# Turning the attended tiles of a gated cross-attention kernel by DMA in two 16-bit planes, with ScalarE joining and VectorE rounding

## Chip, cores and metric

The kernel runs on 1 core of a Trainium2 chip, as one launch. The metric is the device time of that launch in microseconds.

## What is computed

`x` and `ctx` are 64 sequences of 128 positions with 256 features, float32. The block is a gated cross-attention followed by a gated feed-forward layer in which each token uses 4 of 16 blocks.

```python
def attend(Q, K, V):                      # 16 heads of 16 features, causal
    scores = jnp.einsum('bhqd,bhkd->bhqk', q, k) * scale
    scores = jnp.where(causal_mask, scores, jnp.finfo(scores.dtype).min)
    return jnp.einsum('bhqk,bhkd->bhqd', softmax(scores), v)
def ffn(x):                               # 1024 hidden units in 16 blocks of 64
    prob = softmax(x @ w_router + b_router)
    mask = the 4 blocks of highest prob, per token
    h = relu(x @ w1.T + b1)
    return (h * mask) @ w2.T + b2
x = x + tanh(g_xattn) * attend(layernorm(x), ctx, ctx)
x = x + tanh(g_ffn) * ffn(layernorm(x))
```

## The kernel before, in words

The work goes by tiles: tile b is one sequence, 128 positions on the partitions and 256 features in the free dimension. The feed-forward part takes two tiles (a pair) at a time. The program is written out engine by engine. Each engine runs its own list of instructions in order, and the lists are tied by semaphores with constant targets. One loop over `ITERATIONS` (i from -4 to 71) is written on every engine; in iteration i, for example, scores of tile i+1, shifted scores of tile i, the output of attention for tile i-1, the transposes of tile i-2's second normalisation, and the feed-forward part of earlier tiles are issued. Nothing but these lists and waits sets the order of the work.

**Attention.** VectorE takes mean and variance of x (`layernorm_stats`, L622) and POOL makes the reciprocal root of the variance as a power of -0.5 on one number per partition (`rstd_of`, L792: L794 adds epsilon, L796 takes the power). VectorE normalises into `q_pad` (L637). The queries have to be turned so that the features lie on the partitions. From tile 9 on, and from tile 7 on for the keys, this is done without TensorE: POOL splits the float32 numbers into a plane of low and a plane of high 16-bit halves (`query_parts` L815, `key_parts` L807), SyncE issues a transposing DMA of the planes (`queries_spread` L929, `keys_spread` L939), and ScalarE joins the planes again by a copy on 16-bit numbers (`q_joined` L498, `k_joined` L504). Each of these moves 256 KB, 1024 16-bit numbers a partition. TensorE computes the scores (L302, L315), VectorE the row maxima (L647, L649), which travel two tiles later in a spare column of the queries. When ScalarE has joined the queries of tile i+2, SyncE moves the maxima of tile i into the rows of tile i's queries by two small DMAs (`max_row`, L921, issues at L925). Only when they have landed can TensorE compute `shifted_scores(i)` (L332), whose exponentials ScalarE takes (L513). POOL zeroes what is not causal (`causal_weights`, L830), and TensorE multiplies with the values (`attention_out`, L345) into bank M0, from which ScalarE copies (L519). After another turn (L359) VectorE divides, gates and adds x (`attention_added`, L652 to L667) and takes the statistics of the result x2.

**From x2 to the feed-forward part, which is what changes.** POOL makes the root of x2's variance (the same `rstd_of`, at the head of its iteration) and then `x_b` (L873). VectorE normalises x2 into `xn` (`normalised_again`, L672). TensorE turns `xn` by two 128x128 transposes (`x_transposed`, L370) into bank M0. ScalarE copies that bank twice (`x_copies`, in `rest`, the last thing of its iteration before the second hidden part): as float32 into `xT` for the router (L525), and rounded to the reduced type fp32r into `xT_high` (L528). VectorE subtracts the two into `xT_low` one iteration later (`x_parts`, L678). The hidden layer multiplies high by high, low by high and high by low (L411 to L413), and the output layer likewise (L434 to L436).

**The router** runs in even iterations i, for the pair whose second tile is i-3. TensorE makes the logits from `xT` (L381, `router_logits`) ahead of `attention_out`, waiting for `x_copied` of that second tile. ScalarE copies them (L593), TensorE turns them (L389), VectorE picks the blocks (`route`, L713 to L729), ScalarE makes `used` (L544), and in the next, odd, iteration SyncE turns `used` by a transposing DMA (`used_spread`, L965), which stands in its list ahead of `max_row`.

**The order in one iteration**, as far as it matters here:

```python
# SyncE:   used_spread (odd i); max_row(i); queries_spread(i+3); keys_spread(i+3); loads (even i); store (odd i)
# ScalarE: k_joined(i+2); logits copy (even i); out_copied(i-1); exponentials(i); hidden_parts(m);
#          choice (even i); q_joined(i+3); x_copies(i-2); hidden_parts(m+1)
# VectorE: finished; attention_added(i-2); normalised(i+3); row_maximum(i+1); hidden_masked(m);
#          normalised_again(i-2); layernorm_stats(i+4); x_parts(i-3); route (even i); hidden_masked(m+1)
# POOL:    root of x2(i-2); x_b; hidden_low; query_parts; values; key_parts; root of x(i+4);
#          causal_weights(i); hidden_low
```

## Time and profile before

| | us |
|---|---|
| median of 3 runs (694.48 to 695.71) | 695.15 |
| span of the profiled execution | 694.6 |
| PE busy | 671.8 |
| POOL busy | 564.2 |
| VectorE (DVE) busy | 519.7 |
| ScalarE (ACT) busy | 511.9 |

The profile gives for the profiled execution the span from its first to its last instruction; what lies around it is not in it. Busy times are unions over an engine's instructions; matmuls are pipelined and their ends are modelled, so where the price of a matmul matters the distance from one start to the next says more than the duration. DMA-issuing instructions of SyncE stand in its timeline (SPq) with the time that issuing took, and are not counted as busy.

### The profile page before, as it was taken

The numbers are of one execution on the slowest core, as the hardware profiler recorded it, in microseconds if no ns is written. First come the engines' busy times: TensorE is split into PE (matmuls) and PEld (weight loads), VectorE is DVE, ScalarE is ACT, GpSimd is POOL, SyncE is SP. The second block draws the span as 40 slices with busy tenths as digits, with TensorE's granted clock in tenths as the row PEclk, the third lists the DMA queues.
The fourth block names the chain that finished last, engine by engine and source line by source line (L and its number), as shares of the span: only waits on it lengthen the run. The fifth ranks groups of instructions, "written<-read, shape, count | busy, mean of one in ns | idle before, by whom it ended". The sixth has DMA issues, their size and how long they took to land.

```text
span 694.6 us, 30557 instructions
## 1 busy us (share of the span) xinstructions
PE 671.8 (97%) x13072; PEld 623.5 (90%) x13072; DVE 519.7 (75%) x1429; ACT 511.9 (74%) x785; POOL 564.2 (81%) x778
## 2 busy tenths in 40 slices
PE   6779999999999999999999999999999999999998
PEld 5668899999999999999989999999999999999997
DVE  6788877877777787787787787778777777877752
ACT  3657787787787878778778777877877877786642
POOL 5687889889888888988988988898898888886642
PEclk9989999999999999999999999999999999999999
DMA  5322345444335354344444444533533544342010
GB/s 162 95 78 39 83 114 75 106 113 80 95 101 110 86 99 113 79 82 113 113 79 103 105 72 99 114 95 86 113 83 82 110 113 77 75 83 50 20 38 32
DMA packets 161814, 61.90 MB, mean 89 GB/s; under 512 B 135696, under 2 KB 161424, under 8 KB 161680
## 3 DMA queue, kind: packets, MB, share of 16 engines
q1 hardware_dynamic: 160848, 58.38, 37.7%
q8 instruction: 104, 1.70, 1.1%
q10 hardware_dynamic: 832, 1.57, 0.8%
q14 instruction: 30, 0.25, 0.1%
HBM read 19.03 MB, written 8.39 MB: 39 GB/s over the span
## 4 chain that ended last, share of the span: by engine, by line
PE 87%; DVE 4%; POOL 3%; SPq 2%; DMA 1%; issue 1%; ACT 1%; POOLq 0%; DVEq 0%
PE bank L411 10%; PE score_banks L332 10%; PE score_banks L302 8%; PE bank L413 8%; PE bank L412 8%; PE bank L436 8%; PE bank L435 8%; PE bank L434 8%; PE bank L345 8%; PE bank L359 4%; PE bank L370 3%; PE bank L381 1%; PE score_banks L315 1%; DMA qT<-qT 1%; PE bank L389 1%
## 5 line engine op out<-in xcount | busy, mean ns | idle before, releaser
L837 POOL TENSOR_TENSOR h_low<-hid,h_high 128x512 fp32r<-128x512 f32 x128 | 164.8, 1287 | 12.8 <-ACT hid L535 12.6
L709 DVE SCALAR_TENSOR_TENSOR hid<-bank,b_cols,used_all 128x256 f32<-128x256 f32 x248 | 108.2, 478 | 73.0 <-PE bank L413 66.9
L513 ACT ACTIVATE weights<-score_banks 128x1024 f32<-128x1024 f32 x128 | 124.3, 1023 | 40.3 <-PE score_banks L332 40.3
L411 PE MATMUL bank<-xT_high,w_high 128*128 128x256 f32 x496 | 150.7, 304 | 0.3 <-DVE hid L709 0.2
L830 POOL TENSOR_SCALAR_AFFINE_SELECT weights<-weights 128x1024 f32<-128x1024 f32 x128 | 138.3, 1105 | 8.6 <-ACT weights L513 8.2
L413 PE MATMUL bank<-xT_high,w_low 128*128 128x256 f32 x496 | 139.2, 281 | 0.0
L412 PE MATMUL bank<-xT_low,w_high 128*128 128x256 f32 x496 | 139.1, 280 | 0.0
L434 PE MATMUL bank<-w_high,h_high 128*128 128x256 f32 x488 | 137.3, 281 | 0.7 <-POOL h_low L837 0.7
L436 PE MATMUL bank<-w_high,h_low 128*128 128x256 f32 x488 | 138.0, 283 | 0.0
L435 PE MATMUL bank<-w_low,h_high 128*128 128x256 f32 x488 | 137.5, 282 | 0.0
L794 POOL TENSOR_SCALAR ve<-mv 128x1 f32<-128x1 f32 x128 | 34.6, 271 | 89.9 <-DVE mv L620 89.8
L411 PEld LDWEIGHTS bank<-xT_high,w_high 128*128 128x128 f32 x496 | 93.3, 188 | 4.7 <-issue 0.6
L412 PEld LDWEIGHTS bank<-xT_low,w_high 128*128 128x128 f32 x496 | 93.7, 189 | 0.0
L413 PEld LDWEIGHTS bank<-xT_high,w_low 128*128 128x128 f32 x496 | 93.3, 188 | 0.0
L434 PEld LDWEIGHTS bank<-w_high,h_high 128*128 128x128 f32 x488 | 92.0, 189 | 0.9 <-POOL h_low L837 0.9
L436 PEld LDWEIGHTS bank<-w_high,h_low 128*128 128x128 f32 x488 | 91.9, 188 | 0.0
L435 PEld LDWEIGHTS bank<-w_low,h_high 128*128 128x128 f32 x488 | 91.8, 188 | 0.0
L534 ACT ACTIVATE h_high<-hid 128x512 fp32r<-128x512 f32 x128 | 82.4, 644 | 9.2 <-DVE hid L709 9.2
L519 ACT COPY oT<-bank 128x512 f32<-128x512 f32 x64 | 37.6, 587 | 67.1 <-PE bank L345 67.1
L501 ACT COPY qT<-qT_parts 128x1024 uint16<-128x1024 uint16 x57 | 77.6, 1361 | 9.0 <-DMA qT_parts<-q_parts 8.6
L332 PE MATMUL score_banks<-qT,kT 32*128 32x128 f32 x2048 | 76.0, 285 | 7.7 <-DVE q_pad L649 4.3
L332 PEld LDWEIGHTS score_banks<-qT,kT 32*128 32x128 f32 x2048 | 63.8, 188 | 20.8 <-issue 13.9
(102 smaller groups left out, 1508.4 us busy)
## 6 DMA issues: line engine op xcount, KB each, us to landing
x_in<-in_x SPq DMA_DIRECT2D x31, 256.0 KB, 3.3
out_y<-y_out SPq DMA_DIRECT2D x31, 256.0 KB, 2.4
c_in<-in_ctx SPq DMA_DIRECT2D x30, 256.0 KB
qT<-qT SPq DMA_DIRECT2D x128, 4.0 KB
w_stage<-in_w1T ACTq DMA_DIRECT2D x1, 1024.0 KB, 5.9
hid<-in_w2T SPq DMA_DIRECT2D x8, 128.0 KB, 2.7
kT_parts<-k_parts SPq DMA_TRANSPOSE x57, 2.8
qT_parts<-q_parts SPq DMA_TRANSPOSE x57, 2.7
```

The lines of the kernel that those rows point to most:

```text
L332: made = pe.matmul(out=score_banks[:, u, cols], lhsT=kT[rows, s, cols], rhs=qT[rows, s, cols], start=True, stop=True, tile_position=(u * P ...
L411: pe.matmul(out=bank, lhsT=w1_high[:, k, c], rhs=high, start=k == 0, stop=False)
L412: pe.matmul(out=bank, lhsT=w1_high[:, k, c], rhs=low, start=False, stop=False)
L413: made = pe.matmul(out=bank, lhsT=w1_low[:, k, c], rhs=high, start=False, stop=k == KC - 1)
L434: pe.matmul(out=bank[:, 0:D], lhsT=high, rhs=w2_high[:, c, :], start=a, stop=False)
L435: pe.matmul(out=bank[:, 0:D], lhsT=high, rhs=w2_low[:, c, :], start=False, stop=False)
L436: made = pe.matmul(out=bank[:, 0:D], lhsT=low, rhs=w2_high[:, c, :], start=False, stop=z)
L513: act.activation(weights[:, b % 2, half * 2 * HB:(half + 1) * 2 * HB, :].rearrange("p h q -> p (h q)"), score_banks[:, 2 * half:2 * half + ...
L534: act.activation(h_high[:, p % 2, chunks], hid[:, n % 4], ACT.Relu)
L709: dve.scalar_tensor_tensor(hid[:, n % 4, j], hid_bank(n)[:, j * TOKS:(j + 1) * TOKS], b1_cols[:, c:c + 1], used_all[:, p % 2], ALU.add, AL ...
L830: pool.affine_select(out=w, in_=w, compare_op=ALU.is_ge, fill=0.0, base=0, pattern=[[0, 2 * HB], [1, S]], channel_multiplier=-1).then_inc( ...
L837: pool.tensor_tensor(h_low[:, p % 2, chunks], hid[:, n % 4], h_high[:, p % 2, chunks].bitcast(F32), ALU.subtract).then_inc(h_low_made, 1)
```

## The change

- **Turning by DMA.** Tiles 6 to 61 (`x_by_pe` is false) are not turned by TensorE. POOL splits `xn` into two 16-bit planes (`x_split`, behind `key_parts` and ahead of `causal_weights`, waiting for `xn_made`). At the head of the next iteration SyncE issues a transposing DMA of 128x512 16-bit numbers (`x_turned_by_dma`), and ScalarE joins the planes into `xT` (`x_joined`), behind `k_joined` and ahead of the logits' copy. For these tiles both PSUM copies go. Tiles 0 to 5, 62 and 63 are still turned by TensorE and copied to `xT` by ScalarE.
- **Rounding.** For all tiles `xT_high` is now made by VectorE from `xT` in SBUF, in `x_parts`, just ahead of the subtraction; the wait for `hidden_made` moves with it.
- **Roots in pairs.** One POOL step makes the root for x of tile i+4 and for x2 of tile i-2 together, over two columns, at the head of the iteration. The statistics of x are taken one tile earlier (`layernorm_stats(i + 5)`), and the loop starts one iteration earlier.

The diff, cut to its core (declarations of semaphores and shifted set-up conditions are left out):

```diff
...
-half_power = sb("half_power", [P, 1], F32)
+half_power = sb("half_power", [P, 2], F32)
...
-mv1 = sb("mv1", [P, 2, 2], F32)
-ve1 = sb("ve1", [P, 2, 1], F32)
-rstd1 = sb("rstd1", [P, 2, 1], F32)
+mv = sb("mv", [P, 2, 2, 2], F32)
+ve = sb("ve", [P, 2, 2], F32)
+rstd = sb("rstd", [P, 2, 2], F32)
...
-mv2 = sb("mv2", [P, 2, 2], F32)
-ve2 = sb("ve2", [P, 2, 1], F32)
-rstd2 = sb("rstd2", [P, 2, 1], F32)
...
+xn_parts = sb("xn_parts", [P, 2, 2, D], U16)
+xT_parts = sb("xT_parts", [P, 2, 2, KC, S], U16)
...
+x_spread = [sem(f"x_spread{i}") for i in range(2)]
...
+TURNS_BY_PE = 6
 def q_early(b):
...
 def used_pair(i):
...
-FIRST, LAST = -4, N - 1 + OUT_LAG + 1
+FIRST, LAST = -5, N - 1 + OUT_LAG + 1
+def root_of_x(b):
+    return b - 4 - FIRST
+def root_of_x2(b):
+    return b + 2 - FIRST
+def x_by_pe(b):
+    return b < TURNS_BY_PE or b >= N - 2
...
     def attention_out(b):
-        if b >= 2:
-            pe.wait_ge(xT_high_made, b - 1)
-        elif b >= 1:
+        if b >= 2 and x_by_pe(b - 2):
+            pe.wait_ge(x_copied, b - 1)
+        if b >= 1:
...
         else:
-            pe.wait_ge(xT_high_made, b)
+            pe.wait_ge(x_copied, b)
...
             hidden(p, m + 1)
-        if 0 <= i - 2 < N:
+        if 0 <= i - 2 < N and x_by_pe(i - 2):
...
     def x_copies(b):
...
         turned = banks[M0][:, 0:D].rearrange("p (c s) -> p c s", s=S)
-        act.wait_ge(x_turned, b + 1)
+        act.wait_ge(x_turned, b + 1 if b < TURNS_BY_PE else b - (N - 2) + TURNS_BY_PE + 1)
         act.copy(xT[:, :, t, :], turned).then_inc(x_copied, 1)
-        if t == 0 and p >= 2:
-            act.wait_ge(hidden_made, PIECES * (p - 1))
-        act.copy(xT_high[:, p % 2, :, t, :], turned).then_inc(xT_high_made, 1)
+    def x_joined(b):
+        p, t = divmod(b, PAIR)
+        n, slot = divmod(b - TURNS_BY_PE, 2)
+        act.wait_ge(x_spread[slot], 16 * (n + 1))
+        act.wait_ge(xT_low_made, b - 1)
+        act.wait_ge(routed, p)
+        act.copy(xT[:, :, t, :].bitcast(U16).rearrange("p c (s h) -> p h c s", h=2),
+                 xT_parts[:, slot]).then_inc(x_copied, 1)
...
     def hidden_parts(p, m):
...
     def rest(i):
         p, m = hidden_pair(i)
-        if 0 <= i - 2 < N:
+        if 0 <= i - 2 < N and x_by_pe(i - 2):
...
         weights_high(i)
+        if 0 <= i - 3 < N and not x_by_pe(i - 3):
+            x_joined(i - 3)
         if pr is not None:
...
-    def stats_of(source, stats, mv, s, b, stats_made, mean_made):
-        dve.bn_stats(stats[:, s, :], source).then_inc(stats_made, 1)
+    def stats_of(source, stats, kind, b, stats_made, mean_made):
+        dve.bn_stats(stats[:, b % 2, :], source).then_inc(stats_made, 1)
         dve.wait_ge(stats_made, b + 1)
-        dve.bn_aggr(mv[:, s, :], stats[:, s, :]).then_inc(mean_made, 1)
+        dve.bn_aggr(mv[:, b % 2, kind, :], stats[:, b % 2, :]).then_inc(mean_made, 1)
...
     def layernorm_stats(b):
...
             dve.wait_ge(x_landed[slot], 16 * (n + 1))
-        stats_of(x_in[:, b % XS, :], stats1, mv1, b % 2, b, x_stats, x_mean)
+        stats_of(x_in[:, b % XS, :], stats1, 0, b, x_stats, x_mean)
...
     def normalised(b):
         s = b % 2
-        dve.wait_ge(rstd1_made, b + 1)
+        dve.wait_ge(rstd_made, root_of_x(b))
...
         dve.tensor_scalar(q_pad[:, b % QS, :, 0:HD], x_in[:, b % XS, :].rearrange("p (h d) -> p h d", d=HD),
-                          mv1[:, s, 0:1], rstd1[:, s], ALU.subtract, ALU.mult).then_inc(qn_made, 1)
+                          mv[:, s, 0, 0:1], rstd[:, s, 0:1], ALU.subtract, ALU.mult).then_inc(qn_made, 1)
...
     def row_maximum(b):
...
         dve.wait_ge(x2_made, b + 1)
-        stats_of(x2[:, s], stats2, mv2, s, b, x2_stats, x2_mean)
+        stats_of(x2[:, s], stats2, 1, b, x2_stats, x2_mean)
...
     def normalised_again(b):
         s = b % 2
-        dve.wait_ge(rstd2_made, b + 1)
-        dve.tensor_scalar(xn[:, s], x2[:, s], mv2[:, s, 0:1], rstd2[:, s],
+        dve.wait_ge(rstd_made, root_of_x2(b))
+        if b >= 2 and not x_by_pe(b - 2):
+            dve.wait_ge(x_parts_made, b - 2 - TURNS_BY_PE + 1)
+        dve.tensor_scalar(xn[:, s], x2[:, s], mv[:, s, 1, 0:1], rstd[:, s, 1:2],
...
     def x_parts(b):
         p, t = divmod(b, PAIR)
+        dve.wait_ge(x_copied, b + 1)
+        if t == 0 and p >= 2:
+            dve.wait_ge(hidden_made, PIECES * (p - 1))
+        dve.tensor_copy(xT_high[:, p % 2, :, t, :], xT[:, :, t, :]).then_inc(xT_high_made, 1)
...
             normalised_again(i - 2)
-        if 0 <= i + 4 < N:
-            layernorm_stats(i + 4)
-        if i == FIRST:
+        if 0 <= i + 5 < N:
+            layernorm_stats(i + 5)
+        if i == FIRST + 1:
...
 def _(pool):
-    def rstd_of(mv, ve, result, s, b, mean_made, ve_made, rstd_made):
-        pool.wait_ge(mean_made, b + 1)
-        pool.tensor_scalar(ve[:, s], mv[:, s, 1:2], LN_EPS, None, ALU.add).then_inc(ve_made, 1)
-        pool.wait_ge(ve_made, b + 1)
-        pool.tensor_tensor(result[:, s], ve[:, s], half_power[:], ALU.pow).then_inc(rstd_made, 1)
+    def roots(i):
+        s = i % 2
+        from_x, from_x2 = 0 <= i + 4 < N, 0 <= i - 2 < N
+        if from_x:
+            pool.wait_ge(x_mean, i + 4 + 1)
+        if from_x2:
+            pool.wait_ge(x2_mean, i - 2 + 1)
+        kinds = slice(0 if from_x else 1, 2 if from_x2 else 1)
+        pool.tensor_scalar(ve[:, s, kinds], mv[:, s, kinds, 1], LN_EPS, None, ALU.add).then_inc(ve_made, 1)
+        pool.wait_ge(ve_made, i - FIRST)
+        pool.tensor_tensor(rstd[:, s, kinds], ve[:, s, kinds], half_power[:, kinds], ALU.pow).then_inc(rstd_made, 1)
...
     def values(b):
...
                          ).then_inc(q_parts_made, 1)
+    def x_split(b):
+        n, slot = divmod(b - TURNS_BY_PE, 2)
+        pool.wait_ge(xn_made, b + 1)
+        if n >= 1:
+            pool.wait_ge(x_spread[slot], 16 * n)
+        pool.tensor_copy(xn_parts[:, slot], xn[:, b % 2].bitcast(U16).rearrange("p (d l) -> p l d", l=2)
+                         ).then_inc(x_parts_made, 1)
...
     def causal_weights(b):
...
         p, m = hidden_pair(i)
+        if 0 <= i + 4 < N or 0 <= i - 2 < N:
+            if i + 4 == 0:
+                pool.wait_ge(numbers_set, 1)
+            roots(i)
         if 0 <= i - 2 < N:
             b = i - 2
-            rstd_of(mv2, ve2, rstd2, b % 2, b, x2_mean, ve2_made, rstd2_made)
             if b == 0:
...
             key_parts(i + 3)
-        if 0 <= i + 4 < N:
-            if i + 4 == 0:
-                pool.wait_ge(numbers_set, 1)
-            rstd_of(mv1, ve1, rstd1, (i + 4) % 2, i + 4, x_mean, ve1_made, rstd1_made)
+        if 0 <= i - 2 < N and not x_by_pe(i - 2):
+            x_split(i - 2)
         if 0 <= i < N:
...
         weights_low(i)
-        if i == FIRST + 2:
+        if i == FIRST + 3:
             pool.memset(k_parts[:, :, :, :, HD:], 0).then_inc(parts_zeroed, 1)
...
+    def x_turned_by_dma(b):
+        slot = (b - TURNS_BY_PE) % 2
+        if b - 2 >= TURNS_BY_PE:
+            sync.wait_ge(x_copied, b - 1)
+        sync.wait_ge(x_parts_made, b - TURNS_BY_PE + 1)
+        sync.dma_start_transpose(xT_parts[:, slot].rearrange("p l c s -> p (l c) s"),
+                                 xn_parts[:, slot].rearrange("p l d -> p (l d)")).then_inc(x_spread[slot], 16)
     for i in ITERATIONS:
         pu = used_pair(i)
+        if 0 <= i - 3 < N and not x_by_pe(i - 3):
+            x_turned_by_dma(i - 3)
         if pu is not None:
```

## Rows read from the trace of the kernel before

**Rows 1.** The page: span, and busy time of the engines.

```profile
span 694.6 us, 30557 instructions
PE 671.8 (97%) x13072; PEld 623.5 (90%) x13072; DVE 519.7 (75%) x1429; ACT 511.9 (74%) x785; POOL 564.2 (81%) x778
```

**Rows 2.** Stretches: length, busy PE, PEld, DVE, ACT, POOL, granted clock, DMA.

```profile
20.00:50.00 30.00, 21.71 (x628) 17.88 (x628) 24.52 (x46) 18.35 (x32) 22.98 (x35) 0.95 0.25 64
300.00:400.00 100.00, 99.53 (x2010) 92.69 (x2010) 75.88 (x216) 78.15 (x118) 85.99 (x117) 1.00 0.45 99
```

**Rows 3.** Timeline of PE: start us, duration us, what.

```profile
342.91 0.44 PE L370 MATMUL bank<-ident,xn 128*128 128x128 f32 x2
343.11 0.36 PE L411 MATMUL bank<-xT_high,w_high 128*128 128x256 f32 x1
...
353.11 0.44 PE L370 MATMUL bank<-ident,xn 128*128 128x128 f32 x2
353.38 0.33 PE L389 MATMUL bank<-adding,logitT 128*128 128x64 f32 x2
```

**Rows 4.** Groups of instructions: busy us, mean ns | idle us before, releaser.

```profile
L370 PE MATMUL bank<-ident,xn 128*128 128x128 f32 x128 | 28.2, 302 | 1.0 <-DVE xn L672 1.0
L709 DVE SCALAR_TENSOR_TENSOR hid<-bank,b_cols,used_all 128x256 f32<-128x256 f32 x248 | 108.2, 478 | 73.0 <-PE bank L413 66.9
L796 POOL TENSOR_TENSOR rstd<-ve,half_power 128x1 f32<-128x1 f32 x128 | 73.2, 572 | 10.7
L794 POOL TENSOR_SCALAR ve<-mv 128x1 f32<-128x1 f32 x128 | 34.6, 271 | 89.9 <-DVE mv L620 89.8
L811 POOL COPY k_parts<-c_in 128x512 uint16<-128x512 uint16 x57 | 34.9, 613 | 0.0
```

**Rows 5.** The chain of waits up to the shifted scores of tile 35.

```profile
352.46 1.25 SPq L936
353.81 2.41 SPq L946
...
357.46 1.18 SPq L965
358.69 0.57 SPq L925
359.31 3.43 DMA qT<-qT
```

**Rows 6.** Timeline of SyncE's issues, iterations 29 and 51.

```profile
294.41 0.45 SPq L918 DMA_DIRECT2D x_in<-in_x  x1
295.42 1.18 SPq L965 DMA_TRANSPOSE used_all<-used  x1
296.65 1.15 SPq L925 DMA_DIRECT2D qT<-qT  x2
...
523.25 1.15 SPq L925 DMA_DIRECT2D qT<-qT  x2
```

**Rows 7.** Timeline of PE: shifted scores 29 and 51, router's matmuls of iterations 12 and 36.

```profile
300.95 1.17 PE L332 MATMUL score_banks<-qT,kT 32*128 32x128 f32 x32
...
526.18 0.50 PE L332 MATMUL score_banks<-qT,kT 32*128 32x128 f32 x8
...
126.08 0.43 PE L381 MATMUL bank<-xT,w_router 128*32 128x128 f32 x8
...
371.74 0.43 PE L381 MATMUL bank<-xT,w_router 128*32 128x128 f32 x8
```

**Rows 8.** Timeline of ScalarE, iterations 12 and 35 to 36.

```profile
125.60 1.38 ACT L507 COPY kT<-kT_parts 128x1024 uint16<-128x1024 uint16 x1
...
368.10 0.38 ACT L525 COPY xT<-bank 128x256 f32<-128x256 f32 x1
...
368.62 0.66 ACT L534 ACTIVATE h_high<-hid 128x512 fp32r<-128x512 f32 x1
...
369.67 1.38 ACT L507 COPY kT<-kT_parts 128x1024 uint16<-128x1024 uint16 x1
```

**Rows 9.** Who waited for whom: us in total, times, longest us.

```profile
SPq L925 <- ACT qT L501: 46.7, 30, 3.1
DVE q_pad L637 <- POOL rstd L796: 3.9, 5, 1.0
```

**Rows 10.** VectorE's second normalisation: duration ns min/median/max.

```profile
L672 DVE TENSOR_SCALAR xn<-x,mv,rstd x64: 402/406/1179, 31.6 to 664.7; 128x256 f32<-128x256 f32 x64
```

More of the change, by code:

```diff
@@ L178, in build @@
         x2_stats, x2_mean, xn_made = sem("x2_stats"), sem("x2_mean"), sem("xn_made")
-        ve1_made, ve2_made = sem("ve1_made"), sem("ve2_made")
+        ve_made = sem("ve_made")
         xT_low_made, hid_made, y_made = (sem(n) for n in ("xT_low_made", "hid_made", "y_made"))
@@ L190, in build @@
         v_zeroed, v_ones_set, v_levels_set = sem("v_zeroed"), sem("v_ones_set"), sem("v_levels_set")
-        rstd1_made, rstd2_made = sem("rstd1_made"), sem("rstd2_made")
+        rstd_made = sem("rstd_made")
         v_made, weighted, x2_b2_made = (sem(n) for n in ("v_made", "weighted", "x2_b2_made"))
@@ L194, in build @@
             "parts_zeroed", "parts_ones_set", "parts_levels_set", "k_parts_made"))
+        x_parts_made = sem("x_parts_made")
         q_parts_zeroed, q_parts_made = sem("q_parts_zeroed"), sem("q_parts_made")
@@ L557, in _ @@
             act.wait_ge(numbers_set, 2)
-            act.activation(scratch[:], half_power[:], ACT.Exp)
+            act.activation(scratch[:], half_power[:, 0:1], ACT.Exp)
             act.wait_ge(triangle_made, 1)
@@ L775, in _ @@
                     route(pr)
-                if i == FIRST + 1:
+                if i == FIRST + 2:
                     places(2)
@@ L780, in _ @@
                     hidden_masked(p, m + 1)
-                if i == FIRST + 1:
+                if i == FIRST + 2:
                     dve.wait_ge(ident_made, 1)
@@ L901, in _ @@
                                     ).then_inc(parts_levels_set, 1)
-                if i == FIRST + 3:
+                if i == FIRST + 4:
                     pool.memset(q_parts[:, :, :, :, RIDE_COL + 1:], 0).then_inc(q_parts_zeroed, 1)
```

## Prediction

> **What bounds the kernel now.** I read the page first: PE is busy 97% of the span, the other engines 74 to 81% [rows 1]. That is an average, so I looked at stretches. Between 300 and 400 us PE is busy for 99.53 of 100 us at the full granted clock, between 20 and 50 us for 21.71 of 30 [rows 2]. So for about 570 us TensorE is the bound, and what it no longer has to do comes off the span, unless something else arrives late. The first 80 us are a chain across engines.
>
> Then I asked how close the others are. The chain of waits shows one place in steady state where PE was held up: the two short DMAs of `max_row(35)` landed 3.43 us after their issue began, and what led to them was SyncE's own queue, one transposing DMA after another [rows 5]. SyncE's timeline shows that this is a pattern. In odd iterations it issues query parts, key parts, two loads, `used_all`, and only then `max_row`, back to back; issuing a transposing DMA takes it 1.2 us whatever the size, now and then 2.4 us [rows 5, 6].
>
> **PE.** 56 of 64 tiles (6 to 61) lose two transposes. Busy time says 28.2 us for 128 [rows 4], 0.44 us a tile, but matmuls overlap. From start to start it is 342.91 to 343.11, 0.20 us, in front of the hidden matmuls and 353.11 to 353.38, 0.27 us, in front of the logits' turn [rows 3]. Half the tiles are of each kind: 56 x 0.23 = 12.9 us. Bounds: 56 x 0.20 = 11 and 56 x 0.44 = 25 us; starts decide, so I stay near the low end.
>
> **ScalarE.** The two PSUM copies leave the end of the iteration: 368.10 to 368.62, 0.5 us [rows 8]. `x_joined` comes in behind `k_joined`, ahead of the logits' copy, `out_copied` and the exponentials. The like copy of twice the elements takes 1.38 us [rows 8], so it costs 0.7 to 1.4; I take 0.75, near half. For tiles up to 61 the router's matmuls of the even iteration (L381) now wait for it, where before their copy was made an iteration earlier. Usually `k_joined` ends at 371.05 and L381 starts at 371.74 [rows 7, 8]: 0.69 + 0.5 (key copy earlier) - 0.2 (PE earlier) - 0.75 leaves 0.24 us, no stall. But in six of 26 even iterations the query parts landed late and the key copy too: 125.60 + 1.38 = 126.98, against L381 at 126.08 [rows 7, 8]. There the join ends 0.90 - 0.5 + 0.2 + 0.75 = 1.35 us too late. The other five are later by less, so I charge 6 x 1.0 = 6 us. Bounds: 0, and, if the copy took 1.38, 0.4 x 20 + 2.0 x 6 = 20 us.
>
> **SyncE.** 56 more transposing DMAs, 1.2 us of issue each, stand at the head of iteration i, ahead of `used_spread`, `max_row` and the query and key parts. Their own waits are long over: the split is made on POOL an iteration before. In even iterations it hides: `max_row` waits for ScalarE's copy, 46.7 us in 30 times, 1.6 us each [rows 9]. In odd ones the queue has 0.56 us to spare (294.86 to 295.42) in the row shown [rows 6], 0.0 to 0.6 in 25 others and 1.5 in one, so `max_row` moves by 0.6 to 1.2, about 0.9 us, and PE comes 0.2 earlier. From the end of its issue to the use by L332 there are now 297.80 to 300.95, 3.15 us [rows 6, 7]; over the 27 odd iterations from 9 to 61 the gaps are 1.8 to 3.2, median 3.0. That leaves 1.9. How long does the landing take? At most 1.78 us in iteration 51 (524.40 to 526.18, PE did not wait) [rows 6, 7], and 2.9 us in iteration 35 (359.84 to 362.74) [rows 5]. So the charge is 0 in each if landings are of the first kind and 27 x 1.0 = 27 us if of the second. Only one of 27 is shown to have held PE up, so I stay nearer the low end: 0.22 each, 6 us.
>
> The Trainium skill ("DMA: Bandwidth & Descriptors", section "Issuing engines are not separate DMA queues") says that the time to initiate a DMA is usually small beside the DMA. The trace disagrees for this form: 1.25 us of issue. By the page's word SyncE's charge would be nil.
>
> **VectorE.** It now makes all 64 high parts (128x256, SBUF to SBUF), where it only subtracted. The nearest row is the normalisation of the same size, 402 ns at least, 406 median, 1179 at most [rows 10]; I take 0.4, 26 us in all, and at worst 1.2. It lies between `layernorm_stats` and `route` or `hidden_masked`, which idle for PE anyway: 73.0 us in front of L709 alone [rows 4]. Charge 0; if that idle time were gone it would be 26 us. Its new waits (`x_copied`, and `hidden_made`, which moves here from ScalarE) are met in steady state; behind them queue `route` and the second `hidden_masked`.
>
> That 1179 is a VectorE operation held up by POOL. The Trainium skill ("SBUF — State Buffer", section "Who interferes with whom") has copies and casts in a 2-port mode taking a port pair shared with GpSimd, each blocking the other for a whole instruction. The trace agrees in kind; the added copy falls beside POOL's work, so by the rule POOL loses up to 0.4 us an iteration or VectorE about a microsecond, both within idle time.
>
> **POOL.** Two roots of 0.27 + 0.57 us a tile become one [rows 4], over two columns: 0.57 to 1.14 us for the power; I take 0.6, since the fixed part must be most of it. That saves 0.8 us a tile, and the split (128x512 16-bit, like L811's 0.61 us) gives back 0.6. The split waits for `xn_made`, which holds up the causal selects behind it, but leaves them no later than the second root did: nil. The early place of x's root helps at the start, where VectorE waited 3.9 us for it in five tiles [rows 9] and PE was idle: -2 us, bounds 0 and -4.
>
> **Sum.** 12.9 + 2 gained; 6 + 6 lost, less 1 because a router stall gives the next `max_row` time: -3.9 us. The profiled execution spans 694.6 us, the median is 695.15, 0.5 above; the difference goes on the median: 691.2, say 691.
>
> **Rivals.**
> A, forecast: part of PE's gain is given back at `max_row` and the router: 691. Chance 0.42.
> B, hidden anyway: landings are fast and the joins in time, PE keeps it all: 695.15 - 14.9 = 680. For it: only one stall on a DMA in steady state today. Against: the gaps in odd iterations shrink by a third, and six key copies end after L381. The skill's page on DMA, cited above, leans this way. Chance 0.18.
> C, slower: SyncE's queue becomes the bound of the odd iterations. The x transpose pushes `max_row` by 0.9 us, landings behind loads and transposes take 2.9, PE idles in front of L332. With this in half of the 27, 13.5 us, and 6 at the router: 695.15 - 14.9 + 19.5 = 700. It decides from 0.33 us an odd iteration, (14.9 - 6) / 27. For it: rows 5 show just this chain with the transposing DMAs in it, and there will be more slow issues. Against: a typical landing is under 1.8. Chance 0.27.
> D, gain and loss cancel: 0.33 us an odd iteration: 695. Chance 0.13. That the change does not do what it says has no room: the diff takes the transposes off PE.
>
> Range: from 681, which leaves out the lower part of B, to 701, which leaves out the upper part of C (27 us at `max_row` would give 713). A alone, with its two charges between 3 and 9 us each, spans 684 to 697. No change is within 0.2% (693.8 to 696.5), about what a measurement of this kernel can tell. A gives 0.37 faster and 0.03 each for same and slower, less a little; with B, C and D: faster 0.55, same 0.15, slower 0.30.
>
> **What would show it.** PE should show 16 L370-like transposes where there were 128, and L332 should be waiting for the DMA on qT in odd iterations, by 6 us in sum if A is right, near nothing if B, over 13 if C. L381 waiting for ScalarE, 6 us in about six places, shows the router term; in every even iteration it would mean a copy nearer 1.4 us. ScalarE's join should be 0.75 us, VectorE's high part 0.4, POOL's power 0.6. PE should have less idle time between 20 and 50 us by 2 us. If L411 or L434 wait for VectorE or POOL, my zero charges there are wrong; so is the PE term if the step from L332 to L411 grows.

## Result and profile after

The changed kernel takes 704.79 us (median of 4 runs, 702.76 to 705.86), beside 695.43 for the kernel before in the same session (4 runs, 694.48 to 696.61): a ratio of 1.0131, 95% interval 1.0109 to 1.0153. It is slower by 9.4 us where I forecast 4 us faster, and it lies beyond the range's upper end of 701. The profiled execution spans 704.1 us, 9.5 more than that of before [rows 1].

The page after, span, busy times and the queue that SyncE's DMAs use:

```profile
span 704.1 us, 30581 instructions
PE 664.9 (94%) x12960; PEld 615.2 (87%) x12960; DVE 557.0 (79%) x1493; ACT 517.8 (74%) x721; POOL 554.2 (79%) x718
...
q1 hardware_dynamic: 191312, 65.72, 47.5%
```

PE has 112 matmuls fewer and 6.9 us less to do than in [rows 1], and yet the span is longer: PE now waits. Stretches of the kernel after (length, busy PE, PEld, DVE, ACT, POOL, granted clock, DMA), to be read against [rows 2]:

```profile
20.00:50.00 30.00, 22.39 (x632) 19.36 (x631) 23.54 (x44) 17.91 (x29) 20.69 (x27) 0.90 0.15 42
300.00:400.00 100.00, 97.69 (x1987) 90.46 (x1986) 82.79 (x218) 78.49 (x107) 83.59 (x107) 1.00 0.55 108
90.00:645.00 555.00, 539.45 (x10769) 500.71 (x10768) 451.90 (x1226) 437.27 (x590) 462.69 (x587) 1.00 0.56 106
```

The granted clock in the steady part is full, as before. Between 20 and 50 us it is 0.90 on average, against 0.95 in [rows 2]. In the last stretch PE is idle for 15.5 us; in the kernel before it was idle there for 0.5, as its row of the same stretch shows:

```profile
90.00:645.00 555.00, 554.53 (x10989) 517.16 (x10989) 423.30 (x1187) 434.70 (x654) 474.08 (x640) 1.00 0.43 94
```

Who waited for whom after the change (total us, times, longest):

```profile
PEld score_banks L344 <- DMA qT<-qT: 20.0, 25, 2.3
PE score_banks L344 <- DMA qT<-qT: 12.1, 17, 2.0
...
PEld bank L393 <- ACT xT L545: 6.7, 10, 1.1
...
PE bank L393 <- ACT xT L545: 4.6, 9, 0.9
```

L344 is the line of the shifted scores (L332 before) and L393 that of the router's logits (L381 before). Both waits stand where the prediction named them; one is twice as large as I charged.

**Where the 9.5 us are.** The shifted scores of tile 8 and of tile 63 cut the span in three. PE's timeline after:

```profile
87.60 1.17 PE L344 MATMUL score_banks<-qT,kT 32*128 32x128 f32 x32
...
655.62 1.17 PE L344 MATMUL score_banks<-qT,kT 32*128 32x128 f32 x32
```

and before:

```profile
86.43 1.17 PE L332 MATMUL score_banks<-qT,kT 32*128 32x128 f32 x32
...
647.37 1.17 PE L332 MATMUL score_banks<-qT,kT 32*128 32x128 f32 x32
```

The middle takes 568.0 us instead of 560.9, 7.1 more; the start takes 1.2 more and the tail (48.5 against 47.3) 1.2 more. Among the variants below the start goes from 83.8 to 88.3 and the tail from 46.9 to 48.6, so I attribute neither of these two to a cause.

In the middle, the distance between the shifted scores of neighbouring tiles is 10.20 to 10.23 us before and, where nothing stalls, 10.02 to 10.04 after: PE gains 0.18 to 0.19 a tile, about 10.2 us over 55 tiles. Added up from one start to the next over iterations 9 to 63, the stalls in front of L344 are 12.1 us in 19 places, all in odd iterations (before: 0.5 in one), and those in front of L393 5.4 us in 10 places (before: none). So -10.2 + 11.6 + 5.4 = +6.8 of the 7.1 us. Below, "stalls" are these sums for L344 and L393.

**What delays `max_row`.** SyncE's timeline of the kernel after, iteration 39, with what led up to it (start us, issuing time, line):

```profile
399.12 1.25 SPq L977 DMA_TRANSPOSE qT_parts<-q_parts  x1
400.46 2.35 SPq L987 DMA_TRANSPOSE kT_parts<-k_parts  x1
402.90 0.54 SPq L955 DMA_DIRECT2D c_in<-in_ctx  x1
403.50 0.48 SPq L959 DMA_DIRECT2D x_in<-in_x  x1
404.08 1.20 SPq L1014 DMA_TRANSPOSE xT_parts<-xn_parts  x1
405.37 1.20 SPq L1006 DMA_TRANSPOSE used_all<-used  x1
406.62 1.24 SPq L966 DMA_DIRECT2D qT<-qT  x2
```

The seven issues stand back to back. The small spare time in front of `used_all` that [rows 6] show is gone; the added line L1014 comes before it and pushes all behind it. PE's timeline then has, for shifted scores 39 and 47 (the brackets: idle time before, and the releaser):

```profile
410.16 0.39 PE L344 MATMUL score_banks<-qT,kT 32*128 32x128 f32 x4 [1.57 <-DMA qT<-qT]
...
492.33 0.39 PE L344 MATMUL score_banks<-qT,kT 32*128 32x128 f32 x4 [0.17 <-DMA qT<-qT]
```

In iteration 39 issue ends at 407.86 and PE starts 2.30 us later. In iteration 47 the landing is short, and a slow `used_all` makes the delay instead:

```profile
486.57 1.19 SPq L1014 DMA_TRANSPOSE xT_parts<-xn_parts  x1
487.85 2.13 SPq L1006 DMA_TRANSPOSE used_all<-used  x1
490.04 1.15 SPq L966 DMA_DIRECT2D qT<-qT  x2
```

There issue ends at 491.19, and PE starts 1.14 us later. Of the 19 stalls 11 have a landing of 1.7 to 2.5 us (7.3 us of stall), and eight one of about 1.1 (4.8 us). In each of these eight one issue of the x turn or of `used_all` took 2.1 to 3.2 us (four times each), and in no other of the 28 odd iterations did one of the two take 2 us. Measured from the shifted scores of the tile before, the issue of `max_row` in odd iterations ends at 8.43 us after the change and at 7.16 before (medians of 28): it moved by 1.3 us. Where no issue is slow it goes from 7.06 to about 8.16, by 1.1 us.

**What makes the router late.** In seven of the ten stalls at L393 ScalarE had finished the key copy and waited for the x turn itself to land. In iteration 48, for example (start us, duration us, line; the brackets as above):

```profile
498.69 1.36 ACT L519 COPY kT<-kT_parts 128x1024 uint16<-128x1024 uint16 x1
501.25 0.77 ACT L545 COPY xT<-xT_parts 128x512 uint16<-128x512 uint16 x1 [1.20 <-DMA xT_parts<-xn_parts]
```

SyncE had finished issuing that turn at 498.06, 3.19 us before the join started. In eight of the 26 even iterations from 10 to 60 the join waited in this way, each time until 2.9 to 3.4 us behind the end of the issue. In the other three stalls (iterations 12, 24 and 56) the join followed a late key copy, the case that the prediction had priced.

**The other parts.** One tile's or one line's instructions after (duration in ns, min/median/max):

```profile
L1014 SPq DMA_TRANSPOSE xT_parts<-xn_parts x56: 1188/1214/2371, 92.4 to 657.4; - x56
L545 ACT COPY xT<-xT_parts x56: 754/777/796, 98.4 to 660.8; 128x512 uint16<-128x512 uint16 x56
...
L828 POOL TENSOR_TENSOR rstd<-ve,half_power x70: 567/720/734, 5.2 to 670.9; 128x2 f32<-128x2 f32 x58, 128x1 f32<-128x1 f32 x12
```

and, as groups (busy us, mean ns, idle time before and its releaser), the high part, the split and what is left of the transposes:

```profile
L863 POOL COPY xn_parts<-xn 128x512 uint16<-128x512 uint16 x56 | 35.1, 626 | 4.3 <-DVE xn L694 4.3
L702 DVE CAST xT_high<-xT 128x256 fp32r<-128x256 f32 x64 | 26.8, 419 | 0.2 <-issue 0.2
...
L382 PE MATMUL bank<-ident,xn 128*128 128x128 f32 x16 | 3.7, 315 | 0.7 <-DVE xn L694 0.7
```

### The profile page after: what moved, and what is told of

Read it like the earlier page. It is cut to its first block, busy times and chain, and to the rows that moved or that the text cites. A ratio compares the mean times of both kernels' runs of the same rounds, so it can differ in the third digit from the quotient of the medians.

```text
span 704.1 us, 30581 instructions
## 1 busy us (share of the span) xinstructions
PE 664.9 (94%) x12960; PEld 615.2 (87%) x12960; DVE 557.0 (79%) x1493; ACT 517.8 (74%) x721; POOL 554.2 (79%) x718
## 3 DMA queue, kind: packets, MB, share of 16 engines
q1 hardware_dynamic: 191312, 65.72, 47.5%
## 4 chain that ended last, share of the span: by engine, by line
PE 30%; SPq 22%; DVE 14%; DMA 13%; issue 10%; POOL 8%; ACT 2%; POOLq 0%; DVEq 0%
PE score_banks L344 5%; SPq L977 5%; DMA qT<-qT 5%; SPq L987 5%; SPq L1014 4%; PE bank L423 4%; POOL q_parts L854 3%; DMA used_all<-used 3%; SPq L1006 3%; PE bank L425 3%; PE bank L424 3%; PE bank L446 3%; PE bank L447 3%; PE bank L448 3%; POOL x_b L916 2%
## 5 line engine op out<-in xcount | busy, mean ns | idle before, releaser
L448 PE MATMUL bank<-w_high,h_low 128*128 128x256 f32 x488 | 136.2, 279 | 0.0
L344 PE MATMUL score_banks<-qT,kT 32*128 32x128 f32 x2048 | 76.9, 287 | 20.1 <-DMA qT<-qT 12.1
L344 PEld LDWEIGHTS score_banks<-qT,kT 32*128 32x128 f32 x2048 | 64.6, 190 | 34.4 <-DMA qT<-qT 20.0
L552 ACT ACTIVATE h_high<-hid 128x512 fp32r<-128x512 f32 x128 | 80.8, 632 | 10.1 <-DVE hid L735 10.0
L667 DVE TENSOR_REDUCE q_pad<-score_banks 128x8 f32<-128x1024 f32 x64 | 78.1, 1220 | 5.1 <-PE score_banks L327 5.0
L553 ACT ACTIVATE hid<-hid 128x512 f32<-128x512 f32 x128 | 80.5, 629 | 0.0
```

The costliest lines, as they stand in the source:

```text
L344: made = pe.matmul(out=score_banks[:, u, cols], lhsT=kT[rows, s, cols], rhs=qT[rows, s, cols], start=True, stop=True, tile_position=(u * P ...
L448: made = pe.matmul(out=bank[:, 0:D], lhsT=low, rhs=w2_high[:, c, :], start=False, stop=z)
L552: act.activation(h_high[:, p % 2, chunks], hid[:, n % 4], ACT.Relu)
```

## Experiments

Theory S (the place in SyncE's queue): SyncE issues in order, so the added transposing DMA, at 1.2 us of issuing ahead of `max_row`, makes the loss; what is issued behind `max_row` costs nothing. Rivals: the DMA engines' own work (queue share 37.7% before, 47.5% after) slows all landings wherever the added DMA stands (rival D of the expectations, where it is called the rings' work; not the D of the prediction); or the loss comes from VectorE's, POOL's or ScalarE's new work (rival V). The table gives medians, the number of runs, the ratio to the kernel before run beside each, and the stalls of the profiled execution in iterations 9 to 63, under the lines of the changed kernel.

| run | us | runs | ratio, 95% | stalls L344 / L393 |
|---|---|---|---|---|
| e1_all_by_pe | 695.74 | 10 | 0.9991 (0.9973 to 1.0010) | 0.1 / 0 |
| e2_odd_tiles_by_dma | 698.11 | 10 | 1.0024 (0.9999 to 1.0049) | 1.0 / 7.3 |
| e3_idle_small_dmas | 706.34 | 4 | 1.0125 (1.0074 to 1.0175) | 2.3 / 0 |
| e4_idle_turns | 703.13 | 4 | 1.0102 (1.0060 to 1.0144) | 5.0 / 0 |
| e5_odd_turn_behind_max_row | 700.33 | 10 | 1.0061 (1.0040 to 1.0083) | 1.8 / 12.7 |
| e6_and_even_join_first | 699.60 | 10 | 1.0055 (1.0029 to 1.0081) | 5.4 / 7.3 |
| e7_only_even_join_first | 703.08 | 4 | 1.0097 (1.0071 to 1.0123) | 12.0 / 3.3 |
| e8_idle_turns_behind_max_row | 696.29 | 10 | 0.9996 (0.9974 to 1.0018) | 0.2 / 0 |
| e9_even_tiles_behind_max_row | 695.39 | 12 | 0.9992 (0.9973 to 1.0012) | 3.9 / 0 |
| e10_even_tiles_at_the_head | 700.89 | 8 | 1.0068 (1.0041 to 1.0096) | 7.3 / 0 |
| e11_loads_behind_max_row | 702.56 | 6 | 1.0081 (1.0054 to 1.0109) | 0.1 / 13.4 |
| e12_even_tiles_loads_behind | 689.22 | 4 | 0.9891 (0.9853 to 0.9929) | 0.1 / 0 |
| e13_after_loads_behind | 695.80 | 10 | 0.9987 (0.9960 to 1.0015) | 0.1 / 10.1 |
| e14_before_loads_behind | 695.93 | 10 | 0.9986 (0.9964 to 1.0008) | 0.1 / 0 |

The stalls are those of one execution each, and the executions of one kernel differ by up to 8 us here. In e2 and e5 the profiled one was the longest (700.79 and 704.13), in e3 and e11 the shortest (701.04 and 699.94). Something else stands in no stall column: in the profiled executions of e2, e5 and e11 the granted clock fell to half (1.2 GHz) for 3.4 us in the steady part, once in each, within 1.1 us of the end of a stall of 1.9 to 2.0 us at the router. In e11 (the second row is a stretch; its granted clock is 0.51):

```profile
494.75 0.43 PE L393 MATMUL bank<-xT,w_router 128*32 128x128 f32 x8 [2.01 <-ACT xT L545]
...
495.10:498.50 3.40, 3.40 (x68) 3.01 (x60) 0.67 (x2) 1.63 (x3) 1.73 (x4) 0.51 0.59 135
```

In these three the middle is 1.7 to 1.9 us longer than the gain on PE and the two stalls account for, about half of 3.4 us. Where the clock fell, the stall cost more than its own length. One of e14's ten executions took 1570.37 us, which nothing here explains; the median of the other nine is 695.92.

### The change without its DMAs

```diff
-        TURNS_BY_PE = 6
+        TURNS_BY_PE = N
```

> The changed kernel with all 64 tiles turned by TensorE (56 transposing DMAs, splits and joins gone); roots in pairs and VectorE's rounding stay. Theory S (the transposing DMAs cost the 17.5 us of stalls in front of L344 and L393, and the rest of the change is nearly free): about the kernel before, 694 to 698 us, no stall of the shifted scores past iteration 9. Rival V (VectorE's rounding or the early statistics cost by themselves): 699 us or more, with the added time spread over the middle. The 1.2 us lost before iteration 8 and the 1.3 us lost after iteration 63 should stay in either case, as they lie where TensorE turns the tiles.

695.74 against 695.88: no difference. What is left of the change here is VectorE's rounding for all tiles, the roots in pairs and the early statistics of x. In the stretch from 90 to 645 us PE is never idle, though VectorE has 24 us more to do there than before:

```profile
90.00:645.00 555.00, 555.00 (x10999) 517.96 (x10998) 447.07 (x1242) 421.46 (x601) 441.25 (x540) 1.00 0.42 94
```

So these parts cost nothing, and the gain that I expected of the early root isn't there either. Of the 1.2 us at the start and the 1.3 at the end, which I had expected to stay, 0.6 and nothing are left.

### Turning by DMA only the tiles whose turn falls into even iterations

```diff
-            return b < TURNS_BY_PE or b >= N - 2
+            return b < TURNS_BY_PE or b >= N - 2 or b % 2 == 0
```

(Tile b is turned in iteration b+3; the counts of the semaphores follow.)

> The changed kernel with only the 28 odd tiles from 7 to 61 turned by DMA, which SyncE issues in even iterations; even tiles go by TensorE. Theory S (it is the transposing DMA ahead of the row maxima in odd iterations): the 12 us in front of L344 go, about 5 us in front of L393 stay, TensorE saves 28 x 0.18 = 5 us: 697 us. Rival D (it is the load on the DMA rings, wherever it is issued): half of the 12 us stays, about 703 us.

698.11. With no x turn in the odd iterations the stalls at L344 fall from 12.1 to 1.0 us. Those at L393 are all there, 7.3 us, so half the gain on PE (28 x 0.19 = 5.3 us) is more than given back.

### The kernel before with a DMA that nobody reads

Into iterations 9 to 64 of the kernel before, ahead of `used_spread`, went a transposing DMA of 128x512 16-bit numbers (e4), or two DMAs of 4 KB (e3), issued in the same time but moving 8 KB in place of 128 KB. In e8 those of odd iterations stand behind `max_row`.

```diff
             for i in ITERATIONS:
                 pu = used_pair(i)
+                if 6 <= i - 3 < N - 2:          # e3, e4; e8: only i % 2 == 0
+                    idle_dma(i - 3 - 6)
...
                     max_row(i)
+                if 6 <= i - 3 < N - 2 and i % 2 == 1:      # e8 only
+                    idle_dma(i - 3 - 6)
```

> The kernel before with two small DMAs of 4 KB that nobody reads, issued by SyncE at the head of iterations 9 to 64 (1.1 us of issue, hardly any bytes). Nothing of the computation is left out. If the time of issuing is what delays the row maxima, 5 to 8 us are added, 700 to 703 us, with stalls in odd iterations only. If the DMA rings' work is what counts, nothing is added, 695 to 697 us.

> The kernel before with a transposing DMA of 128x512 16-bit numbers that nobody reads, issued at the head of iterations 9 to 64, as the change issues its own. If issuing alone decides, the same as with the two small DMAs within 1.5 us. If the DMA rings' work decides or adds, 708 us or more, the stalls of the changed kernel in front of L332 (12 us) and also a late landing behind the loads: 12 to 14 us over the kernel before.

> The kernel before with the same 56 transposing DMAs that nobody reads, in odd iterations behind the row maxima instead of ahead of them. Same bytes and same time of issuing. Theory S: nothing is lost, 695 to 697 us against 703 at the head. Rival D: as at the head, 701 us or more.

SyncE's timeline shows that e4 and e3 shift `max_row` alike. First e4:

```profile
483.94 1.19 SPq L978 DMA_TRANSPOSE idle_dst<-idle_src  x1
485.22 1.21 SPq L970 DMA_TRANSPOSE used_all<-used  x1
486.48 1.15 SPq L930 DMA_DIRECT2D qT<-qT  x2
```

then e3:

```profile
483.12 1.22 SPq L979 DMA_DIRECT2D idle_dst<-idle_src  x2
484.44 1.20 SPq L970 DMA_TRANSPOSE used_all<-used  x1
485.70 1.24 SPq L930 DMA_DIRECT2D qT<-qT  x2
```

The place decides: the same 56 transposing DMAs cost 7.3 us with all of them at the head (703.13 against 695.88) and nothing with the 28 of odd iterations behind `max_row` (696.29 against 696.36). In e4's profile 4.5 of the added microseconds are at the shifted scores and 3.2 in front of the turn of `xn`; in e8 neither is there. Bytes don't: e3 moves hardly any and costs 10.5 us by its median (e3's and e4's intervals overlap, so which costs more is not settled). e3's time is above what I had written for it. Its profiled execution spans only 699.0, with 2.3 us of stalls at the shifted scores and 1.7 at the turn of `xn` (e4: 5.0 and 3.2), far below its own median of 706.34; its four runs go from 701.04 to 707.73. What the longer ones did isn't in the one that was profiled, and stays open.

### The real change with its odd turns behind `max_row`

```diff
-                if 0 <= i - 3 < N and not x_by_pe(i - 3):
+                if 0 <= i - 3 < N and not x_by_pe(i - 3) and i % 2 == 0:
                     x_turned_by_dma(i - 3)
...
                     max_row(i)
+                if 0 <= i - 3 < N and i % 2 == 1 and not x_by_pe(i - 3):
+                    x_turned_by_dma(i - 3)
```

In odd iterations the join goes behind the exponentials, and the rounding and the subtraction to the end. e6 also puts the even iterations' join ahead of `k_joined`; e7 is the changed kernel with only that.

> The changed kernel with the same 56 transposing DMAs, but in odd iterations SyncE issues its one behind the row maxima; ScalarE joins behind the exponentials there, and VectorE splits at the end of the iteration. Even iterations are as in the changed kernel. Theory S (place in SyncE's queue): the 12 us in front of L344 go, the 5 us in front of the router's matmuls stay: 692 to 694 us. Rival D (the rings' work slows the landings wherever it is issued): at least 6 of the 12 us stay, 699 us or more.

> As the one before, and in even iterations ScalarE joins x ahead of the keys instead of behind them. If the stalls in front of the router's matmuls come from the join standing behind the key copy, 3 to 5 us more go: 687 to 690 us. If they come from late landings of the x planes themselves (4.1 to 4.6 us in ten cases), only 1 to 2 us go: 691 to 692 us.

> The changed kernel with that one edit alone: in even iterations ScalarE joins x ahead of the keys. Theory: the stalls at the row maxima stay (12 us, perhaps a little more, as a router stall gave the next row maxima time), those at the router shrink by 3 to 5 us: 700 to 702 us. If ScalarE's order is not the cause, 704 to 706 us.

e5: L344's stalls fall from 12.1 to 1.8 us, as theory S says, and the time from 704.8 only to 700.33, since L393's grow from 5.4 to 12.7. By its time alone e5 would speak for rival D (699 us or more), but D wanted at least 6 us left at L344. Waits of e5:

```profile
PE bank L393 <- ACT xT L545: 10.9, 26, 1.9
...
PE score_banks L344 <- DMA qT<-qT: 4.1, 5, 1.7
```

Two things make that. Most of the 26 stalls are of only 0.24 us: the late join of the odd iteration delays ScalarE's next key copy by 0.6 us, and the even join behind it. And a stall at L344 had, as I read it, hidden part of the router's lateness: it puts off PE, while SyncE and ScalarE go on. With the join ahead of the key copy (e6) L393 has 7.3 and L344 5.4; 699.60. e7 takes 2.1 us off L393 and leaves L344 at 12.0; 703.08, 1 us above what I wrote. e6 missed what I wrote by 10 us. The router's part was larger than I had counted, and the order on ScalarE is only a part of it: in e7, with the join ahead of the key copy, it still waits for the landing of its own planes in 18 of 26 even iterations.

### Half the tiles by DMA, behind `max_row` or at the head

To take the router out: only even tiles, whose turn falls into odd iterations, go by DMA, the odd ones stay on PE (so the second tile of each pair, for which L393 waits, is copied an iteration earlier, as before). e9 issues them behind `max_row`, with the join and the rounding late in the odd iteration as in e5; e10 issues them at the head, with both where the change has them.

```diff
-            return b < TURNS_BY_PE or b >= N - 2
+            return b < TURNS_BY_PE or b >= N - 2 or b % 2 == 1
```

> Only the 28 even tiles from 6 to 60 by DMA, issued in odd iterations behind the row maxima, joined by ScalarE behind the exponentials and split by VectorE at the end of the iteration; odd tiles, on which the router waits, by TensorE. Theory S: no DMA ahead of the row maxima and no join in front of the router, so no stall at L344 or L393 is left, and TensorE keeps 28 x 0.18 = 5 us: 690 to 692 us, below both kernels. Rival D (the added transposing DMAs cost wherever they stand): 696 us or more.

> The same 28 even tiles by DMA, issued at the head of odd iterations as the change does, ahead of used_spread and the row maxima. Theory S: the stalls in front of L344 are back, 8 to 12 us (less a little, as TensorE runs 0.09 us an iteration less far ahead), none at the router: 699 to 703 us. Rival: if the 12 us need the even iterations' DMAs too, 693 to 696 us.

The place, and what goes with it, is worth 5.5 us here too: 695.39 against 700.89, run side by side. The two profiled executions show 3.7 us of it in the middle, 3.4 at L344. But e9 missed the 690 to 692 that I wrote. It has no stall at L393, yet 3.9 us at L344 and 2.5 us in front of the odd tiles' transposes:

```profile
PE score_banks L353 <- DMA qT<-qT: 4.3, 6, 1.2
...
PE bank L391 <- DVE xn L705: 2.5, 3, 0.9
```

28 turns give PE 28 x 0.2 = 5.6 us, and these two take it back. L353 is still at the mercy of SyncE's queue, in which two loads of 256 KB stand ahead of `used_all`.

### The loads behind `max_row` too

The loads of a pair go from the end of the even iteration to behind `max_row` of the odd one, x a pair earlier so that it is there in time:

```diff
+                if i % 2 == 1 and i - 1 >= 8:
+                    loads_of(i - 1)
...
-                if b >= 2 * PAIR and b % PAIR == 0 and b < N:
-                    load(b // PAIR)
+                if i < 8 and b % PAIR == 0:
+                    loads_of(i)
```

e11 is e6 with this, e12 is e9 with this, e13 is the changed kernel and e14 the kernel before with this and nothing else.

> The kernel of e6 (all 56 tiles by DMA, odd iterations' behind the row maxima, even joins first) with the two loads of 256 KB moved as well: from iteration 8 on they are issued behind the row maxima of the odd iteration, and x is loaded a pair earlier. In front of the row maxima then stand only the queries', the keys' and used_all's transposing DMAs. Theory S with the landings as its second half (2 to 2.5 us behind the loads, 1.1 without): the 5 us left in front of L344 in e6 go, those at the router (7 us) shrink or stay, and the early load takes the wait of the statistics away at the start: 690 to 694 us. Rival D (any added transposing DMA costs): 698 us or more, as e6.

> The kernel of e9 (28 even tiles by DMA, behind the row maxima, odd tiles by TensorE) with the loads moved in the same way. Theory S: the 4 us left in front of the shifted scores in e9 go: 690 to 692 us. Rival D: as e9, 695 us or more.

> The changed kernel, its transposing DMAs where the change puts them, and only the loads moved (behind the row maxima of the odd iteration, x a pair earlier). The queue has 3.25 us of work before used is ready at 4.6 us after the shifted scores, so the x transpose, 1.2 us, fits into the gap that the loads leave. Theory S: no stall in front of L344 from iteration 11 on (12 us gone), the router's stalls of 5 us stay: 692 to 695 us. If the stalls need only the transposing DMA ahead, whatever else stands there, 4 us or more of them stay: 697 us or more.

> The kernel before with only the loads moved in the same way. It has one stall of 0.5 us on the row maxima to win and perhaps 1 us at the start: 694 to 696 us. If it comes to 690 us or less, the gain of e12 is the loads' and not TensorE's 28 tiles.

In all four the stalls at L344 from iteration 9 on are gone, in e13 with every x turn still at the head. e13's SyncE shows why, an odd iteration's issues:

```profile
495.55 1.22 SPq L1018 DMA_TRANSPOSE xT_parts<-xn_parts  x1
497.91 1.31 SPq L1010 DMA_TRANSPOSE used_all<-used  x1
499.27 1.13 SPq L970 DMA_DIRECT2D qT<-qT  x2
500.51 0.39 SPq L955 DMA_DIRECT2D c_in<-in_ctx  x1
500.95 0.46 SPq L963 DMA_DIRECT2D x_in<-in_x  x1
```

Without the two loads ahead of it the x turn is out at 496.77, and `used_all` then waits 1.14 us for `used` and not for the queue. So it takes both, the x turn and the loads (402.90 to 404.08, 1.2 us, in the changed kernel's iteration 39), to make `max_row` late. e13 is 695.80, level with the kernel before: what it still loses is the router's wait, grown to 10.1 us:

```profile
PE bank L393 <- ACT xT L545: 8.7, 16, 1.4
...
PE score_banks L344 <- DMA qT<-qT: 3.1, 2, 1.6
```

(Of the last row's 3.1 us all but 0.1 lies before iteration 9.) I had written 692 to 695 with 5 us of it. The join waits for the x turn's landing in 15 of 26 even iterations here, against 8 in the changed kernel: counted from the shifted scores of the tile before, the turn's issue ends at 5.67 us instead of 5.19 (medians). That those scores came late in the changed kernel, held up at L344, would explain it; no run separates this from the loads' new place. e11 has that wait alone, 13.4 us, and its 702.56 is 9 us above what I wrote. By its time it meets what I had written for rival D (698 or more), so D is refuted only as far as L344 goes, and how much of the router's part is the landing of the turns themselves stays open. Its profiled execution spans 698.2. As with e3, the profiled one is the shorter, and for e13 too (691.6); the difference isn't explained.

e12 has neither wait and takes 689.22 us (4 runs, 688.93 to 689.55), a ratio of 0.9891 to the kernel before: it beats both kernels. The loads alone give nothing (e14, 695.93), and the turns alone gave nothing (e9). PE in e12:

```profile
90.00:645.00 555.00, 554.39 (x11027) 516.75 (x11026) 458.38 (x1245) 434.46 (x604) 455.17 (x571) 1.00 0.48 100
```

PE is full again, with 38 matmuls more in the stretch than before although 56 fewer are to be done in all: it is further on. From the shifted scores of tile 8 to those of tile 63 it takes 554.5 us against 560.9, 6.4 less: 0.5 is the stall of before, and 28 x 0.21 = 5.9 the iterations whose turn is gone (10.02 us instead of 10.23; of these 0.21, 0.03 are there in e1 too, without any DMA).

## Why the prediction was wrong

It went rival C's way: SyncE's queue became the bound of many odd iterations. The landing that the prediction took as typical, of iteration 51, had a slow issue just ahead of it, 2.56 us where 1.18 is usual. This is its row in the kernel before:

```profile
520.64 2.56 SPq L965 DMA_TRANSPOSE used_all<-used  x1
```

By its steps:

- **SyncE: the step that failed.** I charged 0.22 us an odd iteration, 6 us in 27; measured 12.1 us, 0.45 each. Two parts were too small. First, "`max_row` moves by 0.6 to 1.2, about 0.9 us": it moved by 1.3. The spare time was used up as I had reckoned, but POOL's query parts end 0.17 us later (the power over two columns takes 0.15 more), and a few issues take over 2 us: 15 of 146 transposing DMAs before, 20 of 202 after. The prediction had seen such issues and charged nothing for them; the eight stalls with a slow issue of the x turn or `used_all` hold 4.8 us. Second, the landing: "a typical landing is under 1.8" was read from one row, iteration 51, and it was not typical, as the row above shows. After the change just the stalls behind such an issue have the short landing of 1.1 us; in the other 11 the two small DMAs landed 1.7 to 2.5 us behind their issue. With 12.1 in place of 6 my sum would have come to 697.3. e4 against e8 shows that the place ahead of `max_row` is the cause, e10 against e9 agrees, and e13 shows that the loads in the same queue are the other half of it.
- **PE.** "56 x 0.23 = 12.9 us": 0.18 to 0.19 a tile, 10.2 us over 55. The starts, not the durations, were right to go by; my mean of 0.20 and 0.27 was still high. This took 2.7 us from the forecast.
- **ScalarE and the router.** "6 x 1.0 = 6 us": 5.4 us in ten places. The size came out right by luck. The prediction counted late key copies, and only three of the ten are that; in seven the join waited for its own planes to land, 2.9 to 3.4 us behind the issue, a wait that has no term in the sum. With L344's stalls gone the router's are 10 to 13 us (e5, e11, e13). "Leaves 0.24 us, no stall" was thin; the join itself is 0.777 us against 0.75.
- **The start.** "-2 us" is not seen. PE is busy for 22.39 us between 20 and 50, 0.7 more than before, but at a granted clock of 0.90 instead of 0.95, so this isn't more work done, and the shifted scores of tile 8 come at 87.60, not earlier. e1, with all of the early root, is level with the kernel before.
- **VectorE.** Right at nothing: 419 ns a piece on average, and PE's waits for it aren't there in e1.
- **POOL.** 0.72 us a power against my 0.6, the split 0.63 against 0.6. Nothing on the bound but the 0.15 us above.
- **The sum.** -10.2 at PE, +11.6 and +5.4 at the two waits, and +2.4 at the two ends, whose cause is open, give +9.2, of 9.5 in the profiled executions. (By its own working, A's span should begin at 685, not at 684.) C, with 13.5 and 6, had the two waits about right; its 700 was low through the 2 us at the start and the 2.7 at PE.
- **The Trainium skill.** "DMA: Bandwidth & Descriptors", section "Issuing engines are not separate DMA queues", has the time to initiate a DMA as usually small beside the DMA, and by it SyncE's charge would be nil. The runs disagree for this form: 1.2 us of issuing, in odd iterations ahead of `max_row` or behind it, makes the difference between 7.3 us lost (e4) and none (e8).

## What to carry to other kernels

Before a DMA is added to an engine's in-order list, look for the last small transfer in that list that someone waits for, and count all issues ahead of it, of the iteration before too: here 1.2 us of issuing for each transposing DMA, whatever it moved. Put new transfers and loads behind it, and check that two waits that end close together are both cured, since the one may hide the other. Before a typical landing is taken from one row, look at what its neighbours in the queue did in that row. A unit that is 97% busy gives back only what it no longer does from start to start (0.19 us for two transposes), so the time that any neighbour can lose is small. And charge the landing of the new transfer itself to whoever reads it: here ScalarE's join waited for it up to 3.4 us behind the end of its issue.

## What the runs showed of the chip

- The issuing time of a transposing DMA between SBUF tiles didn't go by its size: 1.214 us (median) for 128x512 16-bit numbers, 1.253 for the queries' 128x1024, and two DMAs of 4 KB took 1.22 together. Now and then one took 2.1 to 3.2 us (`used_all`, 3204 ns at most).
- Behind the same list of transfers, the two small DMAs landed 1.1 us behind the end of their issue in the eight stalls where the x turn's or `used_all`'s issue had taken 2.1 to 3.2 us, and 1.7 to 2.5 us behind it in the other 11.
- Where ScalarE waited for it, the transposing DMA of 128x512 16-bit numbers had landed 2.9 to 3.4 us behind the end of its issue in the changed kernel, and in e7 1.3 to 1.7 us in seven places and 1.9 to 3.3 in eleven.
- A power over two columns takes 0.720 us on POOL, over one column 0.567.
- Two DMAs that moved 8 KB in all (e3) cost no less by their median than one that moved 128 KB (e4: 706.34 and 703.13, intervals overlapping), while the same 128 KB, in odd iterations behind `max_row` (e8), cost nothing, though the DMA engines' busy share between 90 and 645 us rose from 0.43 to 0.51 in it.
- The granted clock fell to half for 3.4 us in three profiled executions (e2, e5, e11), each time 0.2 to 1.1 us after PE had been idle for 1.9 to 2.0 us.
